# The scan's skip term, from two diagonal matmuls on TensorE to a row multiply and an addition on VectorE

## The chip, the cores and the metric

The kernel runs on one core of a Trainium2 chip. Its time is the device time of one execution in microseconds; lower is better. Three runs of the kernel before gave 847.05, 847.98 and 848.30 us.

## The reference, cut to what matters

The input has 8 sequences of 512 tokens with 128 channels. Each passes a normalization, then two branches: a Mamba-2 block with an MLP behind it (`s`), and an attention block with a mixture of four experts behind it (`g`); the output is `x + s * silu(g)`. The change touches the Mamba-2 part alone. It has 4 heads of 64 channels (256 in all) and a state of 64 per channel:

```python
xBC = silu(conv(xBC))                  # xs: 4 heads x 64, Bm: 64, Cm: 64
def step(h, inp):                      # over the 512 tokens
    dA = exp(dt_t * A)                 # one number per head
    h = h * dA + (dt_t * x_t) B_t^T
    y = h C_t
y = ys + xs * D[None, None, :, None]   # D: one number per head. The skip connection
y = y * silu(z)
y = y * rsqrt(mean(y**2) + EPS) * norm_w
return y @ out_proj_w.T
```

## The kernel before, in words

The kernel works on one sequence at a time, in rounds. A round has a stage B and a stage A. Stage B(r) carries the tail of sequence r (output projections, experts, MLP) and the head of sequence r+1 (projections, convolution, the attention's maxima). Stage A(r) then does the attention's exponentials and weighted values, the scan, and the normalization of the next input. One loop of 7 rounds runs on each engine's own instruction stream; a round -1 without a tail stands before it and a last stage B behind it. So stage A runs 8 times. The order of work on each engine is written out by hand; engines meet only through semaphores.

Stage A has 24 steps `e`, four groups `g` of six units `u`. Each step is one block of attention scores: TensorE makes the scores (`exp_scores`, L519, and `exp_scores_of_four`, L535, tile `S`), ScalarE exponentiates them into `sb_pr` (L1136), GpSimd masks them (L1784), TensorE weighs the values with them (`weigh_values`, L549, tile `R` from `sb_pr`, `sb_va`). In the first six steps TensorE also makes the scores of which VectorE takes the last maxima (`max_scores`, L487; `maxima`, L1236, record L1242).

Beside each group runs one chunk of 128 tokens of the scan, so there are four chunks, c = g = 0 to 3. All matrices are computed for a chunk at once:

- `scan_inputs` (L606): TensorE turns the chunk's `xact` to tokens by channels, into bank `R[2]` (256 columns of x, 128 of B and C), and the product of B and C into its last 128 columns.
- `scan_products` (L1518): VectorE makes `xdt` = turned x times dt (L1525), copies B (L1528) and masks the product (`gm`, L1529).
- `segments` (L590): TensorE makes the sums of decays in bank `R[1]`; ScalarE exponentiates them into `es` (L1181). The segments of chunk c wait for the state of chunk c-1 (`h_sb`), since they share the bank.
- `scan_weights` (L1531): VectorE multiplies `es` and `gm` to `wm` (L1535).
- GpSimd makes `xw` from `xdt` (L1791), for the new state.
- `scan_outputs` (L619): TensorE writes bank `R[3]`. Columns 256 to 511 get the share of the state (C times `hst`, chunks 1 to 3 alone); columns 0 to 255 get first the skip, `xact` times a diagonal matrix of D (`diag_d`, two products), and on it `wm` times `xdt` for each head.
- `scan_combine` (L1539): VectorE weighs the state's share by `dec` (L1548), adds the rest (L1553) and multiplies by silu(z) into `yz` (L1556). In chunk 0 there is only the last of the three.
- `scan_state` (L1558): VectorE moves the new state into `hst` (L1561 in chunk 0, L1563 and L1568 in the others).
- `turn_y` (L643): TensorE turns `yz` for the output projection (L647).

VectorE's order within stage A is in the function `stage_a` (L1570): a step has, in this order, the combine, the maximum, the attention's values, the scan's products, the scan's weights, the state, then the two early normalizations (`xn`, L1589), the statistics of the next input (L1266, step 9), the sigmoid and the joins of the output (L1499 to L1516) and the norms (L1279). GpSimd's order has besides the masks the norms' powers (L1680 at step 17).

A matmul of fp32 operands appears as two records in the trace, with two weight loads. All records of TensorE made by the helper `mm` have the line L455, so they are told apart by their tiles.

Of the kernel before, what the change touches and what calls it, by code (L numbers as in the profile page):

```python
# [32 lines left out]
ALU = mybir.AluOpType  # L33
# [3 lines left out]
P = 128  # L37
B, L, D = 8, 512, 128
T = L // P
NH, HP, NS = 4, 64, 64  # L40
DI = NH * HP
# [52 lines left out]
def build(nc, x, weights, vectors, rows, consts, out):  # L94
    with ExitStack() as ctx:
        def sb(name, shape, dt=F32):
            return ctx.enter_context(nc.sbuf_tensor("sb_" + name, shape, dt))
# [6 lines left out]
        def signal(name, per_round, ahead=0):  # L104

            sem = ctx.enter_context(nc.semaphore(name))
            per[sem.name], lead[sem.name] = per_round, ahead
            made.append(sem)
            return sem

        def at(sem, r, k):


            return (r + 2 + lead[sem.name]) * per[sem.name] + k
# [9 lines left out]
        ones = cst[:, 3 * P:4 * P]  # L124
# [6 lines left out]
        wqk = sb("wqk", [P, AH, HD])  # L131
        neg_a = sb("neg_a", [P, NH])
        diag_d = sb("diag_d", [P, 2, P])

        def w(name):
            a, b = W_COLS[name]
# [34 lines left out]
        xact = sb("xact", [P, 3, L])  # L171
# [6 lines left out]
        dec = sb("dec", [P, 3, T, NH])  # L178
# [11 lines left out]
        xdt = sb("xdt", [P, 2, DI])  # L190
# [4 lines left out]
        yc = sb("yc", [P, 2, DI])  # L195
# [34 lines left out]
        R = [ps(f"R{i}", [P, L]) for i in range(4)]  # L230
# [20 lines left out]

        pool_set = signal("pool_set", 0)
        dve_set = signal("dve_set", 0)
        act_set = signal("act_set", 0)


# [88 lines left out]
        h1_sb = signal("h1_sb", 2)  # L345
        sv_sb = signal("sv_sb", 1)
        cs_sb = signal("cs_sb", 2)
        moe_sb = signal("moe_sb", T * E)
        gr_sb = signal("gr_sb", 1 + T)
        og_sb = signal("og_sb", 3)  # L350
# [1 line left out]
        xdt_sb = signal("xdt_sb", T)  # L352
        gm_sb = signal("gm_sb", T)
        wm_sb = signal("wm_sb", T)
        yc_sb = signal("yc_sb", 2 * (T - 1))
        yz_sb = signal("yz_sb", T)
        h_sb = signal("h_sb", 1 + 2 * (T - 2))
        stat_sb = signal("stat_sb", 2, 1)
# [94 lines left out]
        def _(pe):  # L453
            def mm(o, lhsT, rhs, start=True, stop=True):
                return pe.matmul(o, lhsT, rhs, start=start, stop=stop, skip_group_check=True)  # L455
# [163 lines left out]
            def scan_outputs(r, c):  # L619

                s = slice(c * P, (c + 1) * P)
                pe.wait_ge(xdt_sb, at(xdt_sb, r, c + 1))
                if c == 0:
                    pe.wait_ge(moe_sb, at(moe_sb, r, 2 * E))
                else:
                    pe.wait_ge(h_sb, at(h_sb, r, 2 * c - 1))
                    pe.wait_ge(ao_sb, at(ao_sb, r, 2 * c))
                    mm(R[3][:, DI:2 * DI], cT[:, s], hst[:], True, False)
                for n in range(2):
                    mm(R[3][:, n * P:(n + 1) * P], xact[:, n, s], diag_d[:, n, :], c == 0 and n == 0, False)  # L630
                pe.wait_ge(wm_sb, at(wm_sb, r, c + 1))
                for h in range(NH):
                    i = mm(R[3][:, h * HP:(h + 1) * HP], wm[:, c % 2, h, :],
                           xdt[:, c % 2, h * HP:(h + 1) * HP], False, True)
                i.then_inc(y_ps, 1)

            def new_state(r, c):
# [297 lines left out]
            pe.wait_ge(xab_sb, at(xab_sb, -2, 1))  # L935
            transposes(R[1], lambda t: xa[:, t, :]).then_inc(xaT_ps, 1)
            pe.wait_ge(wh_loaded, 16)
            pe.wait_ge(xbT_sb, at(xbT_sb, -1, 0))
            project_qkv(-1, 0)
            stage_b(-1, False, True)  # L940
# [278 lines left out]
        def _(dve):  # L1219
# [311 lines left out]
            def scan_weights(r, c):  # L1531
                dve.wait_ge(seg_sb, at(seg_sb, r, c + 1))
                dve.wait_ge(gm_sb, at(gm_sb, r, c + 1))
                dve.wait_ge(y_ps, at(y_ps, r, c - 1))
                stt(out=wm[:, c % 2], in0=es[:, c % 2], scalar=1.0,  # L1535
                    in1=gm[:, c % 2, :].unsqueeze(1).broadcast_to([P, NH, P]),
                    op0=ALU.min, op1=ALU.mult).then_inc(wm_sb, 1)

            def scan_combine(r, c):  # L1539

                dve.wait_ge(y_ps, at(y_ps, r, c + 1))
                dve.wait_ge(zs_sb, at(zs_sb, r, 1))
                dve.wait_ge(yT_ps, at(yT_ps, r, c - 1))
                dve.wait_ge(yss_sb, at(yss_sb, r, c - 1))
                if c == 0:
                    y = R[3][:, 0:DI]
                else:
                    tt(yc[:, 0, :].rearrange("p (h d) -> p h d", h=NH),  # L1548
                       R[3][:, DI:2 * DI].rearrange("p (h d) -> p h d", h=NH),
                       dec[:, 0, c, :].unsqueeze(2).broadcast_to([P, NH, HP]), ALU.mult)\  # L1550
                        .then_inc(yc_sb, 1)
                    dve.wait_ge(yc_sb, at(yc_sb, r, 2 * c - 1))
                    tt(yc[:, 1, :], R[3][:, 0:DI], yc[:, 0, :], ALU.add).then_inc(yc_sb, 1)  # L1553
                    dve.wait_ge(yc_sb, at(yc_sb, r, 2 * c))
                    y = yc[:, 1, :]
                tt(yz[:, c % 2, :], y, zraw[:, c, 0:DI], ALU.mult).then_inc(yz_sb, 1)  # L1556

            def scan_state(r, c):  # L1558
# [70 lines left out]
            dve.wait_ge(act_set, 1)  # L1629
            ts(neg_a[:], neg_a[:], -1.0, None, ALU.mult).then_inc(dve_set, 1)  # L1630
            norms(-2)
            dve.wait_ge(dve_set, 13)
            stage_b(-1, False, True)
            dve.wait_ge(wt_loaded, 16)
# [255 lines left out]
```

## Time and profile before

| | |
|---|---|
| median of three runs | 847.98 us |
| the profiled execution's own time | 848.16 us |
| its span, first to last instruction | 846.4 us |
| TensorE busy | 777.2 us (92%) |
| VectorE busy | 613.7 us (73%) |
| ScalarE busy | 510.2 us (60%) |
| GpSimd busy | 293.8 us (35%) |
| mean granted TensorE clock | 0.990 |

Busy time is an average over stages with different limits. A share of 92% does not say that TensorE decides everywhere; that is read from the chain of waits and from the timeline. In a timeline row the first number is the start, the second the length in us from the first of the merged instructions to the end of the last, `xN` the number merged; a bracket says how long the engine had been idle and what released it.

### The profile page before, as it was taken

The page shows a single profiled execution, that of the slowest core. Times are in us where ns is not written, and L with a number is a line of the kernel's source. Part 1 is how long each engine was busy: PE and PEld are TensorE (multiplying, and loading weights), DVE is VectorE, ACT ScalarE, POOL GpSimd, SP SyncE. Part 2 cuts the span into 40 slices and gives each one's busy share as a digit, 9 for nine tenths or more (in the row PEclk, how much of TensorE's full clock was granted, in tenths as well). Part 3 has the DMA queues.
Part 4 walks back from the last instruction along what each step waited for, and adds up shares of the span by engine and source line. Part 5 has one row for each costly group of instructions (what it writes and reads, how often), then busy time and mean ns, then how long its engine had stood idle before and what let it go on. Part 6 is the DMA issues. An engine that isn't in the chain of part 4 may idle for free.

```text
span 846.4 us, 18186 instructions
## 1 busy us (share of the span) xinstructions
PE 777.2 (92%) x5482; PEld 486.3 (57%) x5482; DVE 613.7 (73%) x1491; ACT 510.2 (60%) x968; POOL 293.8 (35%) x577
## 2 busy tenths in 40 slices
PE   2779999999999999999899999999999999999997
PEld 1555564756547565665647565475556656475646
DVE  2685569785887868787697868878587877978624
ACT  2426784577753775467845677537754678456662
POOL 5413534143512616036240445216160262404400
PEclk9998999999999999999999999999999999999999
DMA  4000000000000000000000000000000000000000
GB/s 169 2 8 15 14 1 2 9 16 26 0 2 13 28 3 0 8 13 26 0 0 8 14 25 0 2 7 27 11 0 8 13 27 0 0 8 14 26 0 13
DMA packets 15145, 11.73 MB, mean 14 GB/s; under 512 B 1040, under 2 KB 13968, under 8 KB 14992
## 3 DMA queue, kind: packets, MB, share of 16 engines
q1 hardware_dynamic: 15120, 11.43, 4.5%
q8 instruction: 12, 0.20, 0.1%
q14 instruction: 13, 0.11, 0.0%
HBM read 7.76 MB, written 2.10 MB: 12 GB/s over the span
## 4 chain that ended last, share of the span: by engine, by line
PE 54%; DVE 18%; issue 12%; ACT 10%; POOL 4%; DVEq 1%; POOLq 0%; ACTq 0%
PE R L455 33%; PE S L455 13%; DVE sb_mx L1242 9%; ACT sb_pr L1136 3%; PE S L460 3%; DVE sb_cv L1260 2%; POOL sb_pr L1784 2%; PE R L573 2%; POOL sb_lnv L1680 2%; PE R L460 1%; DVE sb_x L1478 1%; ACT sb_junk L1053 1%; DVE sb_rqk L1387 1%; ACT sb_sq L1034 1%; PE R L616 1%
## 5 line engine op out<-in xcount | busy, mean ns | idle before, releaser
L1136 ACT ACTIVATE sb_pr<-S 128x768 f32<-128x768 f32 (+1 forms) x192 | 161.9, 886 | 111.8 <-PE S L455 111.8
L1242 DVE TENSOR_REDUCE sb_mx<-S 128x2 f32<-128x256 f32 (+3 forms) x256 | 198.0, 818 | 32.9 <-PE S L455 31.9
L1784 POOL TENSOR_SCALAR_AFFINE_SELECT sb_pr<-sb_pr 128x256 f32<-128x256 f32 (+1 forms) x192 | 98.7, 519 | 145.3 <-ACT sb_pr L1136 144.0
L455 PE MATMUL R<-sb_pr,sb_va 128*32 128x512 f32 (+3 forms) x1024 | 88.8, 441 | 3.4 <-POOL sb_pr L1784 1.2
L455 PE MATMUL R<-sb_W,sb_pr 128*128 128x96 f32 (+1 forms) x512 | 69.5, 276 | 0.0
L455 PE MATMUL R<-sb_xfT,sb_W 128*128 128x512 f32 x144 | 69.2, 602 | 0.0
L1771 POOL TENSOR_TENSOR sb_seg_r<-sb_seg_v,sb_seg_head 128x512 fp32r<-128x512 f32 x8 | 8.3, 1040 | 174.7 <-ACT sb_seg_v L1167 174.7
L455 PE MATMUL S<-sb_kT,sb_qT 32*128 32x256 f32 (+3 forms) x512 | 56.7, 385 | 13.0 <-DVE sb_mx L1242 10.2
L455 PEld LDWEIGHTS R<-sb_W,sb_pr 128*128 128x128 f32 x512 | 63.5, 192 | 3.8 <-issue 3.5
L455 PEld LDWEIGHTS S<-sb_kT,sb_qT 32*128 32x128 f32 x512 | 27.6, 183 | 65.5 <-DVE sb_mx L1242 58.2
L455 PE MATMUL S<-sb_qT,sb_kT 32*128 32x256 f32 (+3 forms) x512 | 56.5, 385 | 7.6 <-ACT sb_pr L1136 7.6
L1478 DVE SCALAR_TENSOR_TENSOR sb_x<-R,sb_wts,sb_x 128x96 f32<-128x96 f32 x128 | 40.7, 318 | 17.4 <-PE R L455 13.0
L455 PEld LDWEIGHTS S<-sb_qT,sb_kT 32*128 32x128 f32 x512 | 27.3, 183 | 42.6 <-ACT sb_pr L1136 22.3
L455 PE MATMUL S<-sb_maskb,sb_identb 128*128 128x128 bf16 (+1 forms) x384 | 49.4, 241 | 0.0
L1230 DVE RECIPROCAL sb_rden<-R 128x16 f32<-128x16 f32 x32 | 8.2, 257 | 49.0 <-PE R L573 38.2
L999 ACT ACTIVATE sb_pr<-R 128x512 f32<-128x512 f32 x32 | 19.1, 598 | 39.3 <-PE R L455 39.2
L455 PEld LDWEIGHTS R<-sb_pr,sb_va 128*32 128x32 f32 x1024 | 23.6, 108 | 27.8 <-POOL sb_pr L1784 9.4
L460 PE MATMUL S<-sb_cst,sb_tokqk 128*128 128x128 f32 x256 | 34.1, 294 | 4.2 <-DVE sb_tokqk L1428 2.2
L1694 POOL TENSOR_TENSOR sb_qk<-sb_qk,sb_wqk 128x512 f32<-128x512 f32 x8 | 10.2, 1270 | 75.6 <-ACT sb_sq L1034 75.6
L455 PEld LDWEIGHTS S<-sb_maskb,sb_identb 128*128 128x128 bf16 x384 | 23.8, 98 | 21.4 <-issue 17.7
L1260 DVE SCALAR_TENSOR_TENSOR sb_cv<-sb_xc,sb_vec,sb_cv 128x512 f32<-128x512 f32 x48 | 34.9, 728 | 0.0
L460 PEld LDWEIGHTS S<-sb_cst,sb_tokqk 128*128 128x128 f32 x256 | 31.0, 152 | 6.4 <-ACT sb_qT L1086 2.8
(230 smaller groups left out, 1726.1 us busy)
## 6 DMA issues: line engine op xcount, KB each, us to landing
sb_xin<-x SPq DMA_DIRECT2D x9, 256.0 KB, 2.8
sb_W<-weights SPq DMA_DIRECT2D x1, 2290.0 KB, 10.4
sb_qT<-sb_mT SPq DMA_DIRECT2D x128, 4.0 KB
sb_xres<-x SPq DMA_DIRECT2D x8, 256.0 KB, 2.8
out<-sb_xres SPq DMA_DIRECT2D x7, 256.0 KB, 2.3
sb_cT<-sb_xact SPq DMA_DIRECT2D x8, 128.0 KB, 2.3
sb_W<-weights SPq DMA_DIRECT2D x1, 514.0 KB, 4.6
sb_cst<-consts SPq DMA_DIRECT2D x1, 328.0 KB, 3.2
```

Source lines behind the costliest of these rows:

```text
L455: return pe.matmul(o, lhsT, rhs, start=start, stop=stop, skip_group_check=True)
L460: i = pe.transpose(o[:, t * P:(t + 1) * P], src(t), ident)
L573: i = pe.transpose(R[3][:, t * P:(t + 1) * P], oT[:, g % 2, t * P:(t + 1) * P], ident)
L616: pe.transpose(R[2][:, n * P:(n + 1) * P], xact[:, n, s], ident)
L999: act.activation(dst, R[k % 4][:, :], func, bias=bias).then_inc(act_up, 1)
L1136: act.activation(pr[:, e % 4, :, 0:n], S[pair_of_exp(e)][:, :, 0:n], ACT.Exp).then_inc(p_sb, 1)
L1242: o = dve.tensor_reduce(mx[:, n // P - 1, g, heads[0]:heads[1] + 1], found[:, :, at_col:at_col + n], AX.X, ALU.max, negate=True)
L1260: stt(out=cv[:, n], in0=xc[:, n, k:k + L], scalar=vcol(V_CONVW + TAPS * n + k), in1=cv[:, n], op0=ALU.mult, op1=ALU.add).then_inc(conv_dve, 1)
L1478: stt(out=x2[:, t, MASKED:D], in0=R[(22 + t) % 4][:, e * OC:(e + 1) * OC], scalar=wts[:, t, e:e + 1], in1=x2[:, t, MASKED:D], op0=ALU.mult ...
L1680: tt(lnv[:, 6:8, :].rearrange("p a t -> p (a t)"), lnv[:, 4:6, :].rearrange("p a t -> p (a t)"), minus_half[:], ALU.pow).then_inc(rn_sb, 1)
L1694: tt(qk[:, :, 0].rearrange("p t h d -> p t (h d)"), qk[:, :, 0].rearrange("p t h d -> p t (h d)"), wqk[:].rearrange("p h d -> p (h d)").un ...
L1784: pool.affine_select(out=keep, in_=keep, compare_op=ALU.is_ge, fill=0.0, base=0, pattern=pattern, channel_multiplier=-1)\
```

## The change

The skip is no longer part of the accumulation in `R[3]`. Before the loop, TensorE multiplies a matrix of ones by `diag_d`, which gives D as a row on all partitions; VectorE copies it to `drow`. In each chunk VectorE multiplies the turned x in `R[2]` by that row into `xd`, right behind `wm`. In chunk 0 the combine adds `xd` to the outputs; in the other chunks the product of the state's share with `dec` becomes four scalar_tensor_tensor, one for each head with 64 columns, that multiply by the head's decay and add `xd`. The first product of the heads starts the bank's accumulation in chunk 0.

```diff
         diag_d = sb("diag_d", [P, 2, P])
+        drow = sb("drow", [P, DI])
+        xd = sb("xd", [P, DI])
...
-                for n in range(2):
-                    mm(R[3][:, n * P:(n + 1) * P], xact[:, n, s], diag_d[:, n, :], c == 0 and n == 0, False)
                 pe.wait_ge(wm_sb, at(wm_sb, r, c + 1))
                 for h in range(NH):
                     i = mm(R[3][:, h * HP:(h + 1) * HP], wm[:, c % 2, h, :],
-                           xdt[:, c % 2, h * HP:(h + 1) * HP], False, True)
+                           xdt[:, c % 2, h * HP:(h + 1) * HP], c == 0 and h == 0, True)
...
             pe.wait_ge(wh_loaded, 16)
+            for n in range(2):
+                i = mm(R[0][:, n * P:(n + 1) * P], ones, diag_d[:, n, :])
+            i.then_inc(drow_ps, 1)
+            pe.wait_ge(drow_set, 1)
             pe.wait_ge(xbT_sb, at(xbT_sb, -1, 0))
             project_qkv(-1, 0)
...
                     in1=gm[:, c % 2, :].unsqueeze(1).broadcast_to([P, NH, P]),
                     op0=ALU.min, op1=ALU.mult).then_inc(wm_sb, 1)
+                tt(xd[:], R[2][:, 0:DI], drow[:], ALU.mult).then_inc(xd_sb, 1)
...
-                if c == 0:
-                    y = R[3][:, 0:DI]
-                else:
-                    tt(yc[:, 0, :].rearrange("p (h d) -> p h d", h=NH),
-                       R[3][:, DI:2 * DI].rearrange("p (h d) -> p h d", h=NH),
-                       dec[:, 0, c, :].unsqueeze(2).broadcast_to([P, NH, HP]), ALU.mult)\
-                        .then_inc(yc_sb, 1)
-                    dve.wait_ge(yc_sb, at(yc_sb, r, 2 * c - 1))
-                    tt(yc[:, 1, :], R[3][:, 0:DI], yc[:, 0, :], ALU.add).then_inc(yc_sb, 1)
+                skip = xd[:]
+                dve.wait_ge(xd_sb, at(xd_sb, r, c + 1))
+                if c > 0:
+                    for h in range(NH):
+                        hs = slice(h * HP, (h + 1) * HP)
+                        i = stt(out=yc[:, 0, hs], in0=R[3][:, DI + h * HP:DI + (h + 1) * HP],
+                                scalar=dec[:, 0, c, h:h + 1], in1=xd[:, hs], op0=ALU.mult, op1=ALU.add)
+                    i.then_inc(yc_sb, 1)
                     dve.wait_ge(yc_sb, at(yc_sb, r, 2 * c))
-                    y = yc[:, 1, :]
+                    skip = yc[:, 0, :]
+                tt(yc[:, 1, :], R[3][:, 0:DI], skip, ALU.add).then_inc(yc_sb, 1)
+                dve.wait_ge(yc_sb, at(yc_sb, r, 2 * c + 1))
+                y = yc[:, 1, :]
                 tt(yz[:, c % 2, :], y, zraw[:, c, 0:DI], ALU.mult).then_inc(yz_sb, 1)
...
             norms(-2)
+            dve.wait_ge(drow_ps, 1)
+            dve.tensor_copy(drow[:], R[0][:, 0:DI]).then_inc(drow_set, 1)
+            dve.wait_ge(drow_set, 1)
```

## Rows read from the trace of the kernel before

**Rows 1.** The page, busy time of each engine, share of the span, instructions.

```profile
PE 777.2 (92%) x5482; PEld 486.3 (57%) x5482; DVE 613.7 (73%) x1491; ACT 510.2 (60%) x968; POOL 293.8 (35%) x577
```

**Rows 2.** The page, the chain that ended last, by engine.

```profile
PE 54%; DVE 18%; issue 12%; ACT 10%; POOL 4%; DVEq 1%; POOLq 0%; ACTq 0%
```

**Rows 3.** Groups by line and form: count, busy us, mean ns, idle before.

```profile
L455 PE MATMUL R<-sb_diag_d,sb_xact 128*128 128x128 f32 x128 | 19.5, 275 | 0.0
...
L1548 DVE TENSOR_TENSOR sb_yc<-R,sb_dec 128x256 f32<-128x256 f32 x24 | 10.2, 425 | 20.8 <-PE R L455 19.8
...
L1373 DVE SCALAR_TENSOR_TENSOR sb_x<-R,sb_ry,sb_xn 128x128 f32<-128x128 f32 x32 | 9.0, 345 | 15.5 <-PE R L455 15.5
```

**Rows 4.** Timeline, VectorE instructions out of PSUM: start us, length us.

```profile
379.98 0.42 DVE L1525 TENSOR_TENSOR sb_xdt<-R,sb_dt 128x256 f32<-128x256 f32 x1
380.32 0.21 DVE L1528 COPY sb_btok<-R 128x64 f32<-128x64 f32 x1
...
406.74 1.13 DVE L1373 SCALAR_TENSOR_TENSOR sb_x<-R,sb_ry,sb_xn 128x128 f32<-128x128 f32 x4 [2.02 <-PE R L455]
```

**Rows 5.** Timeline, chunk 0 of one round.

```profile
369.54 0.95 DVE L1242 TENSOR_REDUCE sb_mx<-S 128x2 f32<-128x768 f32 x1
...
370.55 0.45 PE L455 MATMUL S<-sb_kT,sb_qT 32*128 32x256 f32 x4
...
371.15 0.61 PE L455 MATMUL R<-sb_diag_d,sb_xact 128*128 128x128 f32 x4
...
371.60 1.00 PE L455 MATMUL R<-sb_xdt,sb_wm 128*128 128x64 f32 x8
...
372.80 0.42 DVE L1556 TENSOR_TENSOR sb_yz<-R,sb_zraw 128x256 f32<-128x256 f32 x1
...
373.35 1.02 DVE L1242 TENSOR_REDUCE sb_mx<-S 128x2 f32<-128x512 f32 x2
...
374.60 0.51 PE L455 MATMUL S<-sb_qT,sb_kT 32*128 32x512 f32 x4
```

**Rows 6.** Timeline, chunk 1 of the same round.

```profile
380.83 0.82 DVE L1535 SCALAR_TENSOR_TENSOR sb_wm<-sb_es,sb_gm 128x512 f32<-128x512 f32 x1
...
381.62 0.61 PE L455 MATMUL R<-sb_diag_d,sb_xact 128*128 128x128 f32 x4
...
383.10 0.43 DVE L1548 TENSOR_TENSOR sb_yc<-R,sb_dec 128x256 f32<-128x256 f32 x1
...
384.81 0.42 DVE L1568 TENSOR_TENSOR sb_hst<-R,sb_hdec 64x256 f32<-64x256 f32 x1
...
385.28 0.50 PE L455 MATMUL R<-sb_seg_r,sb_seg_l 128*128 128x512 f32 x1
...
386.12 0.45 PE L455 MATMUL S<-sb_qT,sb_kT 32*128 32x384 f32 x4 [0.34 <-ACT sb_pr L1136]
...
386.70 1.06 PE L455 MATMUL R<-sb_pr,sb_va 128*32 128x512 f32 x8
```

**Rows 7.** Timeline, chunk 2 of the same round.

```profile
387.73 0.69 DVE L1512 TENSOR_TENSOR sb_gs<-sb_x,sb_gs 128x512 f32<-128x512 f32 x1
...
389.45 0.61 POOL L1791 TENSOR_TENSOR sb_xw<-sb_xdt,sb_dec 128x256 f32<-128x256 f32 x1 [0.25 <-DVE sb_xdt L1525]
...
390.32 1.83 POOL L1784 TENSOR_SCALAR_AFFINE_SELECT sb_pr<-sb_pr 128x512 f32<-128x512 f32 x2 [0.25 <-ACT sb_pr L1136]
...
392.12 1.64 POOL L1680 TENSOR_TENSOR sb_lnv<-sb_lnv,sb_minus_half 128x8 f32<-128x8 f32 x1
```

**Rows 8.** Timeline, the end of chunk 3 of the same round.

```profile
402.83 0.41 PE L647 MATMUL R<-sb_cst,sb_yz 128*128 128x128 f32 x2
```

**Rows 9.** Timeline, the first projection of the execution.

```profile
16.62 4.94 PE L455 MATMUL S<-sb_W,sb_xbT 128*128 128x384 f32 x8 [1.54 <-ACT sb_xbT L993]
```

**Rows 10.** Windows: us, busy of PE, PEld, DVE, ACT, POOL, granted clock, DMA share, GB/s.

```profile
312.00:316.00 4.00, 2.75 (x15) 1.76 (x14) 3.73 (x11) 3.15 (x15) 0.00 (x0) 1.00 0.00 0
316.00:320.00 4.00, 3.62 (x21) 3.19 (x20) 2.90 (x10) 4.00 (x8) 1.35 (x4) 0.73 0.00 0
```

More of the change, by code:

```diff
@@ L253, in build @@
         dve_set = signal("dve_set", 0)
+        drow_ps = signal("drow_ps", 0)
+        drow_set = signal("drow_set", 0)
         act_set = signal("act_set", 0)
@@ L347, in build @@
         cs_sb = signal("cs_sb", 2)
+        xd_sb = signal("xd_sb", T)
         moe_sb = signal("moe_sb", T * E)
@@ L354, in build @@
         wm_sb = signal("wm_sb", T)
-        yc_sb = signal("yc_sb", 2 * (T - 1))
+        yc_sb = signal("yc_sb", 1 + 2 * (T - 1))
         yz_sb = signal("yz_sb", T)
```

## The prediction

> **What bounds the kernel now.** I read the page's busy shares first. TensorE works 777.2 of 846.4 us and VectorE 613.7 [rows 1]; a change that takes work from the fuller engine and gives it to the emptier one looks good by that row alone. The chain of waits is the better guide: TensorE holds 54% of it, VectorE 18%, issue 12%, ScalarE 10% [rows 2]. So more than a third of the time is set by something other than TensorE. The question is whether the scan is in that part. For that I went through the timeline of one round's stage A, chunk by chunk, asking at each TensorE instruction what came last ahead of it. The round whose stage A lies at 363 to 403 us stands for all eight.
>
> **What is removed.** A 128x128 fp32 matmul is two records, so the skip is 4 records a chunk, 128 in all, 19.5 us busy by the records' own lengths [rows 3]. They overlap, however. In chunk 0 the four start at 371.15 and the next product starts at 371.60 [rows 5]: 0.45 us of TensorE's stream per chunk, 4 x 8 x 0.45 = 14.4 us in all. That is the most that can be gained.
>
> **What is added on VectorE.** Price by start-to-start distance, not by length. Each chunk gets `xd`, a 256-wide product out of PSUM. The 256-wide product of L1525 starts at 379.98 and the next independent instruction at 380.32 [rows 4]: 0.34 us. Chunk 0 gets one more 256-wide addition that the weighing waits for. I price it at its 0.425 us length [rows 3] plus some 0.035 us for the wait (chunk 0's L1556 is as long): 0.46 us. In chunks 1 to 3 one 256-wide product of 0.425 us becomes four 64-wide scalar_tensor_tensor. No row has that form at 64 columns. Four of them at 128 columns take 1.13 us [rows 4], one 0.345 us [rows 3], so the distance is (1.13 - 0.345) / 3 = 0.262 us; 64 columns fewer take 0.07 us off, an estimate from (0.425 - 0.21) us for 256 against 64 columns, a third of it (L1548 [rows 3], L1528 [rows 4]: 0.072). That gives a distance of 0.195 and a length of 0.275 us; four last 3 x 0.195 + 0.275 = 0.86 us, 0.44 more than now. Bounds: at a distance of 0.13 us (0.34 for 256 columns less 3 x 0.07) 0.67 us, and at 0.345 us (a full 128-wide length, nothing overlapped) 1.31 us. I take 0.86, from the nearest row in kind. Per round VectorE gets 4 x 0.34 + 0.46 + 3 x 0.44 = 3.1 us, 25 us in all: 1.7 times what TensorE loses.
>
> The rows show an independent VectorE instruction starting 0.08 us before the one in front has ended (0.42 long, 0.34 apart) [rows 4]. The Trainium skill, "VectorE: DVE Perf Modes", section "The DRAIN you can't avoid", says that the next instruction does not start until the pipe is empty, and its rules advise to lower the number of instructions. The trace disagrees with the first and agrees with the second; the four slices would by the first be 4 x 0.275 = 1.10 us, which is a rival below. In the same page, section "The TRN2 errata", a VectorE instruction out of PSUM is given 120 cycles plus its columns at 0.96 GHz; an estimate from that page makes four 64-wide ones 0.77 us against 0.39 for one of 256, +0.38 where I take +0.44.
>
> **Chunk 0.** After `wm`, VectorE starts the maximum of L1242 at 369.54 and it ends at 370.49; TensorE's next maximum scores, which wait for it, start at 370.55 [rows 5]. There is no slack, so `xd` (+0.34) moves both. TensorE then gets 0.45 us back by the missing skip and is on time again, but the next maximum on VectorE is +0.34, and it was followed by two `xn` instructions, the combine at 372.80 and the last maximum at 373.35 [rows 5]. VectorE could have started that one at 372.80 + 0.34 = 373.14, so 0.21 us of slack. With the extra addition: 0.34 + 0.46 - 0.21 = 0.59 late, end at 374.96 in place of 374.37. The exponent's scores at 374.60 [rows 5] wait for it; they had 374.60 - 374.37 - 0.06 (the wait's own time, as 370.49 to 370.55) = 0.17 us of slack. Chunk 0: +0.42 us.
>
> **Chunk 1.** TensorE gains 0.35 us (the outputs would start at 381.62, the skip's place, but `wm` ends at 380.83 + 0.82 = 381.65 and they wait 0.09 us for it [rows 6]). VectorE is solid from `xdt` to the new state: it inserts `xd` ahead of the statistics, +0.34, less 0.13 us that it idled before 383.10 [rows 6], and the slices +0.44. The state `hst`, 384.81 + 0.42 = 385.23 before, comes 0.65 us later, at 385.88. The segments (385.28 [rows 6]) wait for it, and behind them in TensorE's queue stand the scores at 386.12, held by ScalarE. They would follow the segments by about 0.5 us, at 386.42: +0.30. The values at 386.70 [rows 6] were held by GpSimd, 386.70 - (386.12 + 0.45) = 0.13 us later than the scores alone would have it: +0.15 us. So what TensorE gained is not only lost, the sign turns.
>
> **Chunk 2.** VectorE enters it with its two joins; L1512 starts at 387.73 and has no gap ahead of or behind it [rows 7], so the 0.65 us stay. `xdt` comes at about 389.6, and GpSimd's `xw`, which waits for it (389.45 to 390.06 before), ends at 390.7, after the affine select that starts at 390.32 should have begun [rows 7]. Behind it in GpSimd's queue are a second select and the power at 392.12, which lies on the chain of waits. The two selects take 1.83 us beside VectorE's L1516; in part they will now lie elsewhere. Between 0 and +0.45 us beyond chunk 1; I take +0.15. The 0.45 us of TensorE buy nothing here, since GpSimd sets the end.
>
> **Chunk 3.** The outputs are done 0.44 us earlier, the slices take 0.44 more, and `yz`, which the turning of y at 402.83 waits for, ends where it did [rows 8]. 0 us.
>
> **Start.** Two small matmuls, a copy and a wait come before the first projection at 16.62, which waits 1.5 us for ScalarE's `xbT` [rows 9]; the new work lies beside that. 0 to 0.2 us. If that cover were gone it would cost about 1.3 us, once.
>
> **Sum.** 0.42 + 0.15 + 0.15 = 0.72 us a round, 8 rounds: 5.8 us. The profiled execution took 848.16 us (span 846.4 and 1.76 around it), 0.18 above the median: 848.16 + 5.8 = 854.0 us.
>
> **The clock.** In one round of the profile TensorE is granted 0.73 of its full clock over 316 to 320 us, so half of that stretch was at 1.2 GHz; in the 4 us before it worked 2.75 us of 4 [rows 10]. Were TensorE the bound there, it would cost 4 x 0.27 = 1.1 us. The change shifts stage B against such stretches, so one or two may come fewer or more: -2.2 to +2.2 us, no part of the sum.
>
> **Rivals.**
> A. *TensorE decides, VectorE's additions are covered.* For it: the busy shares [rows 1]. Against it: in chunks 0 and 1 the waits above have slack under 0.2 us. It would give -0.1 (the maximum's 370.55 still holds), -0.35, 0 (GpSimd) and -0.4 us in the four chunks, -0.85 x 8 = -6.8: 841.4 us. It holds from the point where `xd` starts behind the maximum and not ahead of it, or VectorE's idle time before 383.10 exceeds 0.8 us. Chance 0.08.
> B. *The ties are looser than I read.* The 0.1 to 0.2 us slacks are each 0.1 larger and chunk 2's shift is absorbed: +0.2 in chunk 0, 0 after: 1.6 us, 849.8 us; with one low-clock stretch fewer, 848.7. Chance 0.17.
> C. *Slices end to end.* Each slice starts only when the one in front has ended, 0.275 us apart: +0.24 in each of chunks 1 to 3, all on the path: 8 x 0.72 = 5.8 more, 860 us. At 0.345 us it would be 8 x 3 x 0.45 = 10.8 more, 865 us. Against it, the distances in rows 4. Chance 0.12. This is what the Trainium skill's section on the DRAIN, named above, would have.
> D. *GpSimd pays fully in chunk 2*, +0.45 and not +0.15: 2.4 us more, 856.4. I count it within the forecast.
> That the change does not do what it says, I exclude: the skip's matmuls are gone from the code.
>
> **How the numbers follow.** Forecast (with D) 0.63, C 0.12, B 0.17, A 0.08. About 0.2%, 1.7 us, is what a measurement can tell from no change. Slower: all of the forecast and C, and half of B: 0.82. Same: the other half of B: 0.10. Faster: A: 0.08. The range reaches from B's middle, 849, to C's, 860.
>
> **What would show it.** Right: TensorE's idle before the maximum scores of chunk 0 grows by 0.3 us; the segments of chunk 1 wait for `hst`; `xw` starts late in chunk 2; a round 0.7 us longer; VectorE busy near 639 us. Wrong: `xd` under 0.3 us apart from its follower, the slices under 0.15 or over 0.25 us apart, or a stage A of unchanged length.

## The result and the profile after

The kernel after takes 851.72 us in the median of 8 runs (849.91 to 854.22), the kernel before beside it 847.93 (8 runs, 847.05 to 850.01). The ratio is 1.0049, 95% interval 1.0035 to 1.0063: slower by half a per cent. The profiled execution of after took 853.07 us (span 851.3, mean granted clock 0.990). That is 4.9 us above the profiled execution of before, where the medians are 3.8 apart. One program's single runs spread by some 4 us with the granted clock (0.986 in the run of 854.22, 0.995 in that of 849.91), so below I go by rounds in which the clock did not fall.

The page of after, busy time by engine, which answers to [rows 1]:

```profile
PE 772.5 (91%) x5358; PEld 471.3 (55%) x5358; DVE 634.2 (75%) x1604; ACT 511.5 (60%) x968; POOL 298.2 (35%) x577
```

TensorE lost 4.7 us and VectorE gained 20.5. The prediction had 25 us for VectorE (busy near 639 us, 634.2 measured); 2.3 of the missing us are the third join of the output, which got shorter in seven rounds (below). GpSimd, whose instructions are the same 577, gained 4.4 us: some of them take longer now.

The groups by line and form of after, where the new instructions and GpSimd's narrow mask stand (count, busy us, mean ns, idle before):

```profile
L1558 DVE SCALAR_TENSOR_TENSOR sb_yc<-R,sb_dec,sb_xd 128x64 f32<-128x64 f32 x96 | 20.7, 278 | 11.1 <-PE R L460 11.1
...
L1545 DVE TENSOR_TENSOR sb_xd<-R,sb_drow 128x256 f32<-128x256 f32 x32 | 13.3, 415 | 0.0
...
L1797 POOL TENSOR_SCALAR_AFFINE_SELECT sb_pr<-sb_pr 128x256 f32<-128x256 f32 x128 | 58.8, 461 | 102.9 <-ACT sb_pr L1143 102.8
```

A slice takes 278 ns (275 predicted), `xd` 415 (by its distance 340). The same narrow select took 415 ns in the kernel before: no line of it was changed, it only lies beside other work, mostly the first two joins. (A join is one of three 512-wide VectorE instructions with both inputs in SBUF that put the output together; steps 13 and 15.)

**By rounds.** I measure a round from one turning of the attention's values at the start of stage B to the next. An undisturbed round is 98.54 us before (four of the seven lie at 98.41 to 98.56, one at 98.83) and 99.16 after (six of the seven lie at 99.02 to 99.25): +0.62. The profiled difference of 4.91 splits into +0.62 up to the first mark, +2.57 over the seven rounds and +1.71 behind the last mark. Seven times 0.62 is 4.3; to it comes 1.1 of a round of after with a fallen clock, and 2.7 goes off since before had two such rounds; that leaves 2.7, and the small differences between rounds of before make it 2.57. The tail has a fallen clock in after alone.

The +0.62 up to the first mark is another thing than a round's. The first projection starts at 16.62 us in both kernels, but the first stage A starts at 66.43 before and at 66.76 after, +0.33, and is itself only 0.29 us longer. That stage A has no tail and so no joins, and its chunk 2 got shorter: 8.92 us before, 8.70 after.

**By chunk.** The timeline of after in the round shown before. Its stage A starts 1.25 us later (`scan_inputs` of chunk 0 at 366.45 for 365.20), so take 1.25 off to set a start beside [rows 5 to 8]. Chunk 0:

```profile
370.80 0.42 DVE L1545 TENSOR_TENSOR sb_xd<-R,sb_drow 128x256 f32<-128x256 f32 x1
371.13 0.95 DVE L1249 TENSOR_REDUCE sb_mx<-S 128x2 f32<-128x768 f32 x1
...
372.14 0.45 PE L460 MATMUL S<-sb_kT,sb_qT 32*128 32x256 f32 x4 [0.23 <-DVE sb_mx L1249]
...
374.39 0.42 DVE L1563 TENSOR_TENSOR sb_yc<-R,sb_xd 128x256 f32<-128x256 f32 x1
374.85 0.42 DVE L1566 TENSOR_TENSOR sb_yz<-sb_yc,sb_zraw 128x256 f32<-128x256 f32 x1
375.19 1.01 DVE L1249 TENSOR_REDUCE sb_mx<-S 128x2 f32<-128x512 f32 x2
376.26 0.51 PE L460 MATMUL S<-sb_qT,sb_kT 32*128 32x512 f32 x4
```

The maximum scores at 370.89 (372.14 less 1.25) were at 370.55 [rows 5]: +0.34, and TensorE now idles 0.23 us for the maximum. The exponent's scores at 375.01 were at 374.60: +0.41. Chunk 1:

```profile
382.48 0.82 DVE L1542 SCALAR_TENSOR_TENSOR sb_wm<-sb_es,sb_gm 128x512 f32<-128x512 f32 x1
...
383.36 1.10 PE L460 MATMUL R<-sb_xdt,sb_wm 128*128 128x64 f32 x8
...
384.89 0.86 DVE L1558 SCALAR_TENSOR_TENSOR sb_yc<-R,sb_dec,sb_xd 128x64 f32<-128x64 f32 x4
...
387.03 0.42 DVE L1578 TENSOR_TENSOR sb_hst<-R,sb_hdec 64x256 f32<-64x256 f32 x1
387.50 0.49 PE L460 MATMUL R<-sb_seg_r,sb_seg_l 128*128 128x512 f32 x1 [0.34 <-DVE sb_hst L1578]
...
387.93 0.44 PE L460 MATMUL S<-sb_qT,sb_kT 32*128 32x384 f32 x4
388.30 1.07 PE L460 MATMUL R<-sb_pr,sb_va 128*32 128x512 f32 x8
```

The four slices take 0.86 us, 0.19 apart. The segments wait 0.34 us for the state. But the scores follow the segments by 0.43 and the values follow the scores by 0.37, where they had stood 0.84 and 0.58 apart: the slack swallows nearly all. Chunk 2, VectorE's joins, GpSimd's queue and the three places where TensorE waits:

```profile
389.95 0.71 DVE L1519 TENSOR_TENSOR sb_gs<-sb_x,sb_gs 128x512 f32<-128x512 f32 x1
...
391.57 0.61 POOL L1804 TENSOR_TENSOR sb_xw<-sb_xdt,sb_dec 128x256 f32<-128x256 f32 x1 [0.65 <-DVE sb_xdt L1532]
...
391.92 0.82 DVE L1542 SCALAR_TENSOR_TENSOR sb_wm<-sb_es,sb_gm 128x512 f32<-128x512 f32 x1
392.14 2.13 POOL L1797 TENSOR_SCALAR_AFFINE_SELECT sb_pr<-sb_pr 128x512 f32<-128x512 f32 x2
392.79 1.10 PE L460 MATMUL R<-sb_xdt,sb_wm 128*128 128x64 f32 x8 [0.33 <-DVE sb_wm L1542]
392.99 0.78 DVE L1523 TENSOR_TENSOR sb_xres<-sb_gs,sb_xres 128x512 f32<-128x512 f32 x1
...
394.24 1.64 POOL L1693 TENSOR_TENSOR sb_lnv<-sb_lnv,sb_minus_half 128x8 f32<-128x8 f32 x1
...
396.63 0.47 PE L460 MATMUL R<-sb_seg_r,sb_seg_l 128*128 128x512 f32 x1 [0.43 <-DVE sb_hst L1578]
397.68 1.06 PE L460 MATMUL R<-sb_pr,sb_va 128*32 128x512 f32 x8 [0.20 <-POOL sb_pr L1797]
```

The same places in the kernel before (its weights `wm`, the outputs, the segments and the values; rows that stood in no group):

```profile
389.79 0.82 DVE L1535 SCALAR_TENSOR_TENSOR sb_wm<-sb_es,sb_gm 128x512 f32<-128x512 f32 x1
...
391.01 1.00 PE L455 MATMUL R<-sb_xdt,sb_wm 128*128 128x64 f32 x8
...
394.32 0.47 PE L455 MATMUL R<-sb_seg_r,sb_seg_l 128*128 128x512 f32 x1
...
395.69 1.06 PE L455 MATMUL R<-sb_pr,sb_va 128*32 128x512 f32 x8 [0.18 <-POOL sb_pr L1784]
```

GpSimd is late: its selects begin 0.57 us later (392.14 less 1.25 against 390.32 [rows 7]) and take 2.13 us instead of 1.83. But TensorE's outputs wait for VectorE, 0.33 us for `wm`, and its segments 0.43 us for the state (0.14 before, too short for a bracket); only the last values wait for GpSimd, 0.20 us against 0.18 before. The round shown and one other have a chunk 2 of 9.38 us; in the other five rounds of the loop and behind it, where that last wait is 0.10 us, it is 9.25 to 9.27. Chunk 3, its last answer to [rows 8]:

```profile
404.78 0.44 PE L650 MATMUL R<-sb_cst,sb_yz 128*128 128x128 f32 x2 [0.24 <-DVE sb_yz L1566]
```

All kernels in one table. "Round" is an undisturbed one; c0 to c3 are the four parts of stage A in the round shown (cut where chunk 0's scan inputs start and then at each turning of the attention's values, which stands right ahead of the next chunk's inputs; for e4 in the round behind it, since in the one shown its clock had fallen). Chunk 2 of after and of e3 is 9.25 to 9.28 in most rounds. Medians in us with the number of runs; ratios to the kernel before on the same chip, whose medians there were 848.33 (e1 to e4), 848.1 (e5 to e8) and 848.46 (e9 to e12).

| kernel | round | c0 | c1 | c2 | c3 | median (runs) | ratio [95%] |
|---|---|---|---|---|---|---|---|
| before | 98.54 | 13.53 | 8.97 | 8.99 | 6.69 | 847.93 (8) | |
| after | 99.16 | 13.93 | 8.92 | 9.38 | 6.68 | 851.72 (8) | 1.0049 [1.0035, 1.0063] |
| e1 no skip at all | 97.49 | 13.42 | 8.71 | 8.75 | 6.25 | 845.01 (7) | 0.9939 [0.9914, 0.9965] |
| e2 before, unused xd | 98.92 | 13.87 | 8.97 | 9.03 | 6.68 | 848.66 (10) | 1.0004 [0.9991, 1.0017] |
| e3 after, xd later | 98.80 | 13.61 | 8.90 | 9.38 | 6.68 | 848.62 (10) | 1.0001 [0.9990, 1.0012] |
| e4 after, one product | 98.41 | 13.93 | 8.71 | 9.18 | 6.24 | 848.34 (10) | 0.9989 [0.9974, 1.0003] |
| e5 e3, statistics and joins moved | 98.79 | 13.60 | 8.71 | 8.70 | 7.41 | 847.92 (10) | 0.9998 [0.9987, 1.0009] |
| e6 before, both moved | 99.01 | 13.54 | 8.96 | 9.47 | 6.69 | 850.75 (10) | 1.0025 [1.0013, 1.0037] |
| e7 after, joins moved | 99.32 | 13.93 | 8.92 | 8.74 | 7.40 | 852.91 (3) | 1.0047 [1.0027, 1.0066] |
| e8 e3, statistics moved | 98.54 | 13.60 | 8.71 | 9.22 | 6.68 | 848.64 (8) | 0.9994 [0.9981, 1.0008] |
| e9 e8, one join moved, filler | 98.52 | 13.59 | 8.70 | 9.22 | 6.68 | 849.17 (10) | 1.0000 [0.9991, 1.0010] |
| e10 before, filler | 98.55 | | | | | 848.49 (10) | 0.9998 [0.9987, 1.0010] |
| e11 after, filler | 99.13 | | | | | 851.51 (10) | 1.0043 [1.0028, 1.0058] |
| e12 before, e9's moves, filler | 99.06 | 13.55 | 8.97 | 9.50 | 6.69 | 850.97 (10) | 1.0025 [1.0011, 1.0039] |

### The profile page after: what moved, and what is told of

Read it like the earlier page. It is cut to its first block and busy times, and to the rows that moved or that the text cites. A ratio compares the mean times of both kernels' runs of the same rounds, so it can differ in the third digit from the quotient of the medians.

```text
span 851.3 us, 18101 instructions
## 1 busy us (share of the span) xinstructions
PE 772.5 (91%) x5358; PEld 471.3 (55%) x5358; DVE 634.2 (75%) x1604; ACT 511.5 (60%) x968; POOL 298.2 (35%) x577
## 5 line engine op out<-in xcount | busy, mean ns | idle before, releaser
L1797 POOL TENSOR_SCALAR_AFFINE_SELECT sb_pr<-sb_pr 128x256 f32<-128x256 f32 (+1 forms) x192 | 106.8, 561 | 142.3 <-ACT sb_pr L1143 142.0
L460 PEld LDWEIGHTS R<-sb_xdt,sb_wm 128*128 128x128 f32 x256 | 31.7, 191 | 8.5 <-DVE sb_wm L1542 8.0
L460 PE MATMUL R<-sb_xdt,sb_wm 128*128 128x64 f32 x256 | 33.7, 275 | 2.3 <-DVE sb_wm L1542 2.3
L465 PE MATMUL S<-sb_cst,sb_tokqk 128*128 128x128 f32 x256 | 31.2, 276 | 4.8 <-ACT sb_qT L1093 2.3
```

The costliest lines, as they stand in the source:

```text
L465: i = pe.transpose(o[:, t * P:(t + 1) * P], src(t), ident)
L1797: pool.affine_select(out=keep, in_=keep, compare_op=ALU.is_ge, fill=0.0, base=0, pattern=pattern, channel_multiplier=-1)\
```

## The experiments

**e1: what is the matmuls' going worth by itself?** The skip is left out of the kernel before.

```diff
-                for n in range(2):
-                    mm(R[3][:, n * P:(n + 1) * P], xact[:, n, s], diag_d[:, n, :], c == 0 and n == 0, False)
```

> The kernel before with the skip's two matmuls left out and nothing put in their place (the skip term is missing from the result). It prices what TensorE's relief is worth by itself. Theory (short slacks on VectorE and GpSimd decide): the undisturbed round, 98.54 us before, falls by 0.8 to 0.9 us, to 97.7: 0.1 in chunk 0, 0.35 in chunk 1, nothing in chunk 2 where GpSimd's power sets the end, 0.4 in chunk 3; about 841 us. Rival A (TensorE decides everywhere): it falls by the whole 4 x 0.45 = 1.8 us, to 96.8, 834 us. Rival V (VectorE decides everywhere): no change, 848 us.

A round is 1.05 us shorter, each chunk 0.11 to 0.44: a little more than expected, and the 0.24 of chunk 2 was not expected at all, there where I had held GpSimd to set the end. The median is 845.01 and not 841; the clock of the single runs is told at the end. Nothing new lies on VectorE, and this is what rival A would have kept of the 1.8 us of TensorE's stream. In chunk 3 `yz` now comes early enough, and the values are turned 0.44 us sooner.

From before to e1 it is -1.05, from e1 to after +1.67: VectorE's additions cost 1.67 us of the 3.1 they occupy.

**e2: what does `xd` cost where it stands?** The kernel before with its matmuls, and an `xd` that nobody reads.

```diff
                     op0=ALU.min, op1=ALU.mult).then_inc(wm_sb, 1)
+                tt(xd[:], R[2][:, 0:DI], cst[:, P:P + DI], ALU.mult).then_inc(xd_sb, 1)
```

> The kernel before with the skip still on TensorE; VectorE makes in each chunk, at the place of xd, a 256-wide product of the turned x that nobody reads. It adds 4 x 0.34 us a round to VectorE and takes nothing from TensorE. Theory: chunk 0 +0.34 us (the maximum behind it has no slack), chunk 1 close to 0, chunk 2 between 0 and +0.4 by GpSimd's xw, chunk 3 nothing: the undisturbed round +0.35 to +0.7, about 851 to 853 us. Rival A (TensorE decides): no change, 848 us.

+0.38 a round, 0.34 of it in chunk 0. The timeline of e2 (its stage A starts 0.48 us after that of before):

```profile
370.04 0.42 DVE L1540 TENSOR_TENSOR sb_xd<-R,sb_cst 128x256 f32<-128x256 f32 x1
370.37 0.95 DVE L1244 TENSOR_REDUCE sb_mx<-S 128x2 f32<-128x768 f32 x1
371.37 0.44 PE L457 MATMUL S<-sb_kT,sb_qT 32*128 32x256 f32 x4 [0.34 <-DVE sb_mx L1244]
```

`xd` puts the maximum off by 0.33 us (370.37 less 0.48 against 369.54 [rows 5]) and TensorE waits for it: the tie of chunk 0 is as tight as read. In chunks 1 to 3 an `xd` by itself is nearly free (0, +0.04, -0.01). The round is as expected, the median is not: 0.33 us above before, where 8 x 0.38 would give 3.0. The granted clock was 0.988 to 0.994 here and 0.984 to 0.991 in before's runs beside it.

**e3: is its place the cause?** After, with chunk 0's `xd` behind the maximum and two of the `xn`, where VectorE had slack.

```diff
+                if c:
+                    skip_term()
+
+            def skip_term():
                 tt(xd[:], R[2][:, 0:DI], drow[:], ALU.mult).then_inc(xd_sb, 1)
...
+                    if e == 3:
+                        skip_term()
```

> The changed kernel, only chunk 0's xd moved behind the maximum and the two xn of step 3, where VectorE idled 0.35 us. Theory: chunk 0's +0.41 us falls to about +0.1, the undisturbed round from 99.16 to 98.85, 849.5 us at the same clock. Rival (chunk 0's loss comes from the extra addition and not from where xd stands): no change, 99.16.

Chunk 0 falls from 13.93 to 13.61, the round by 0.36. The timeline of e3:

```profile
371.21 0.95 DVE L1249 TENSOR_REDUCE sb_mx<-S 128x2 f32<-128x768 f32 x1
...
372.22 0.45 PE L460 MATMUL S<-sb_kT,sb_qT 32*128 32x256 f32 x4
372.59 0.42 DVE L1549 TENSOR_TENSOR sb_xd<-R,sb_drow 128x256 f32<-128x256 f32 x1
373.03 1.02 DVE L1249 TENSOR_REDUCE sb_mx<-S 128x2 f32<-128x512 f32 x2
```

TensorE's scores no longer wait in this row. With one instruction elsewhere more than half of the loss is gone, 0.36 of 0.62, and the median is level with before.

**e4: what do the four slices cost?** After, with the single product of before in chunks 1 to 3.

```diff
                 if c > 0:
-                    for h in range(NH):
-                        hs = slice(h * HP, (h + 1) * HP)
-                        i = stt(out=yc[:, 0, hs], in0=R[3][:, DI + h * HP:DI + (h + 1) * HP],
-                                scalar=dec[:, 0, c, h:h + 1], in1=xd[:, hs], op0=ALU.mult, op1=ALU.add)
-                    i.then_inc(yc_sb, 1)
+                    tt(yc[:, 0, :].rearrange("p (h d) -> p h d", h=NH),
+                       R[3][:, DI:2 * DI].rearrange("p (h d) -> p h d", h=NH),
+                       dec[:, 0, c, :].unsqueeze(2).broadcast_to([P, NH, HP]), ALU.mult)\
+                        .then_inc(yc_sb, 1)
```

> The changed kernel with the four 64-wide slices of chunks 1 to 3 replaced by the one 256-wide product of before, so the skip term is missing there; xd is still made. It prices the slices: VectorE 0.43 us less in each of three chunks. Theory: chunk 1 gains 0.2 to 0.3 (the segments' wait for the state goes), chunk 2 0.2 to 0.4 (VectorE and xw earlier), chunk 3 0.4 (yz earlier): the undisturbed round from 99.16 to 98.2, about 844 us. Rival G (only GpSimd's late xw counts, chunk 3 is covered): to 98.8. Rival C0 (the loss is all chunk 0): no change.

-0.75 a round, a little less than the 0.96 expected: 0.21, 0.20 and 0.44 in the three chunks by the table, 0.09 in chunk 2 in most rounds. So chunk 1 does pay for its slices, and the 0 of chunk 3 is made of +0.44 for them and -0.44 for the matmuls. The median shows less than 8 times 0.75, since in the profiled execution every second round had a fallen clock and was 1.1 us longer. GpSimd's selects in chunk 2 of another round of e4:

```profile
490.90 2.13 POOL L1796 TENSOR_SCALAR_AFFINE_SELECT sb_pr<-sb_pr 128x512 f32<-128x512 f32 x2
```

The selects stay at 2.13 us without the slices, so another thing stretches them.

**e5 to e8: what stretches chunk 2, and can it be avoided?** The suspects are VectorE's three joins. The first two stand ahead of chunk 2's `xdt` in VectorE's order, the third lies beside the selects. e7 moves them behind the last chunk's combine, in after; e5 does that with e3's place of `xd` and with the statistics of the next input at step 7; e8 is e5 without the joins' move; e6 gives both moves to the kernel before.

```diff
-JOIN_AT = {13: (0, 1), 15: (2,)}
+JOIN_AT = {19: (0, 1, 2)}
-STATS_AT = 9
+STATS_AT = 7
```

> The changed kernel with three moves on VectorE alone: chunk 0's xd behind the maximum (as in the run before), the statistics from step 9 to step 7 (VectorE idled 2 us there) and the three joins from steps 13 and 15 to step 19 (it idled 2 us there too). No instruction more or fewer. Theory: chunk 0 about +0.1 against before, chunk 1 -0.35 (the state is no longer late), chunk 2 -0.3 to -0.5 (xw on time, the selects alone), chunk 3 0: the undisturbed round 97.7 to 98.0, so 842 to 844 us at an undisturbed clock. Rival (the moved work makes VectorE late elsewhere, above all in chunk 3): 98.8 or more.

> The kernel before, skip on TensorE, with the same two moves of the statistics and the joins. Theory: TensorE and ScalarE set the end where VectorE now has room, so next to nothing: undisturbed round 98.3 to 98.6. Then the skip's move is worth about -0.6 us a round in this order of work, where it costs +0.6 in the given one. Rival (the gain of the run above is all the moves' own): 97.8 as well.

> The changed kernel with the three joins alone moved to step 19. Theory: VectorE enters chunk 2 0.6 us earlier, xw is on time and the two selects take about 1.4 and not 2.1 us, so chunk 2's +0.4 us goes: undisturbed round 98.5 to 98.75. Rival (chunk 2's loss is the clock's or TensorE's, not GpSimd's): 99.16 unchanged.

> The changed kernel with chunk 0's xd behind the maximum and the statistics at step 7, joins where they were. Theory: chunk 1's state comes about 0.7 us earlier and VectorE enters the joins earlier, so chunk 2's shift shrinks too: undisturbed round from 98.80 to 98.2 to 98.5. Rival (only the joins count): 98.80 unchanged.

e7 against after: chunk 2 -0.64 (-0.54 in most rounds), chunk 3 +0.72. The joins' place was the cause, as the first stage A had hinted, and moving them only moves the loss: e7's round is 0.16 us longer, where a gain of about 0.5 was expected, and e5 came out at its rival's 98.79. The timeline of e7 in chunks 2 and 3:

```profile
391.79 0.82 DVE L1542 SCALAR_TENSOR_TENSOR sb_wm<-sb_es,sb_gm 128x512 f32<-128x512 f32 x1
...
392.66 1.10 PE L460 MATMUL R<-sb_xdt,sb_wm 128*128 128x64 f32 x8
...
402.28 1.10 PE L460 MATMUL R<-sb_xdt,sb_wm 128*128 128x64 f32 x8 [0.46 <-DVE sb_wm L1542]
```

The scan's inputs of chunk 2 start at 390.19 in e7 and at 389.79 in after. The outputs start 2.48 us behind them in e7 and wait for nothing; in after it is 3.00, with the wait for `wm`. These 0.52 us are the gain. In chunk 3 it is the other way round: there the joins now stand ahead of `xdt`, and TensorE waits 0.46 us for `wm`, where after has no wait. So the joins cost by making VectorE late.

**What stretches the selects** is a second thing. The pair in e5, with the joins gone:

```profile
390.19 1.38 POOL L1803 TENSOR_SCALAR_AFFINE_SELECT sb_pr<-sb_pr 128x512 f32<-128x512 f32 x2 [0.25 <-ACT sb_pr L1143]
```

It takes 1.38 us there, 1.83 in before and 2.13 in after. e9, below, has the first two joins in place and only the third one gone:

```profile
388.31 0.82 DVE L1544 SCALAR_TENSOR_TENSOR sb_wm<-sb_es,sb_gm 128x512 f32<-128x512 f32 x1
388.53 1.68 POOL L1805 TENSOR_SCALAR_AFFINE_SELECT sb_pr<-sb_pr 128x512 f32<-128x512 f32 x2
...
389.18 1.10 PE L460 MATMUL R<-sb_xdt,sb_wm 128*128 128x64 f32 x8 [0.33 <-DVE sb_wm L1544]
...
390.18 1.64 POOL L1701 TENSOR_TENSOR sb_lnv<-sb_lnv,sb_minus_half 128x8 f32<-128x8 f32 x1
```

So the third join is worth 2.13 - 1.68 = 0.45 us of the pair, and the same in before (1.83 - 1.38). The 0.30 us that after adds is `wm`, also a VectorE product of two SBUF inputs: the pair lies beside it for 0.60 us in after and e9 and for 0.29 or 0.30 in before and e5 (389.79 + 0.82 less 390.32), since `wm` came 0.53 us later in the chunk than in before and the selects only 0.23. The third join takes 0.68 us alone, 0.78 in after and 1.12 in before, where it starts inside a select:

```profile
390.54 1.12 DVE L1516 TENSOR_TENSOR sb_xres<-sb_gs,sb_xres 128x512 f32<-128x512 f32 x1
```

And the pair's length is worth next to nothing here: e9 differs from e8 by the third join (and a filler that changes no round, below), its power comes 0.44 us earlier in the chunk, and chunk 2 is 9.19 to 9.23 in both.

e8's earlier statistics gain 0.19 in chunk 1 and 0.05 in chunk 2 (0.16 in the round shown) against e3, since the state comes sooner: 98.54 a round, before's own and just short of what was expected. e6 was a miss. I had expected next to nothing, and the moves cost the kernel before 0.47 a round, all of it in chunk 2: a select beside the first join, for which TensorE waits (as in e12 below):

```profile
395.57 1.06 PE L455 MATMUL R<-sb_pr,sb_va 128*32 128x512 f32 x8 [0.69 <-POOL sb_pr L1784]
```

In the moved order the skip on VectorE (with chunk 0's `xd` behind the maximum) is the faster one, 98.79 against 99.01; in the given order it is slower, 98.80 against 98.54 with `xd` there and 99.16 where the change had put it.

**e9 to e12: one join later, and the clock.** In before the fallen clock lies mostly in stage B, where TensorE idles 0.93 us for the second normalization. The filler gives it two matmuls that nobody reads.

```diff
                 if tail:
+                    if head:
+                        dense(R[0][:, 0:256], 2)
                     pe.wait_ge(x1n_sb, at(x1n_sb, r, 1))
```

e9 has it with e8's order and the third join alone at step 19, e10 with before, e11 with after, e12 with before and e9's two moved constants:

```diff
-JOIN_AT = {13: (0, 1), 15: (2,)}
+JOIN_AT = {13: (0, 1), 19: (2,)}
-STATS_AT = 9
+STATS_AT = 7
```

> The changed kernel with chunk 0's xd behind the maximum, the statistics at step 7, the first two joins where they were and only the third at step 19, behind the norms and outside chunk 2; and two idle 256-wide matmuls of constants into a free bank ahead of TensorE's wait for x1n in stage B, 0.75 us in a gap of 0.93 us, so that they delay nothing. Theory: the third join no longer lies beside GpSimd's two selects of chunk 2 (1.4 us, not 1.8 to 2.1), so the undisturbed round is 98.1 to 98.4, where 98.54 stood without these two edits; and the stretches of low clock in stage B go or get rare, so all runs lie near 843 to 845 us. Rival (the clock falls for another reason than that gap): single runs still 1.3 us apart in steps, clock 0.988 to 0.992, median over 847.

> The kernel before with only the two idle matmuls ahead of the wait for x1n. Theory: undisturbed round 98.54 as before, but the one or two low-clock rounds go: 846 us and less spread. Rival (gap is not the cause): 848, unchanged.

> The changed kernel with only the two idle matmuls. Theory: undisturbed round 99.16; without low-clock rounds the run takes 8 x 0.61 = 4.9 us more than the kernel before with the same two matmuls, some 851 us. Rival: the change costs the measured 3.8 us whatever the clock does.

> The kernel before (skip on TensorE) with the same moves of the statistics and the third join and the same two idle matmuls. Theory: it has no late state in chunk 1, so the statistics bring nothing or cost up to 0.2 us; the third join gives back up to 0.3 us in chunk 2: undisturbed round 98.3 to 98.6, at or above that of the changed kernel with the same moves by 0 to 0.4 us. Rival (the moves alone make the gain, the skip's place none): lower than that of the changed kernel.

The filler changes nothing: e10 and e11 repeat before and after, round and median, and the fallen stretches stay. So the gap it fills is not their cause. The third join gains nothing beyond e8 either, so e9 (98.52 a round, 849.17 us) missed both its round and its time; what is late in its chunk 2 is `wm` (above) and the state once more:

```profile
393.02 0.47 PE L460 MATMUL R<-sb_seg_r,sb_seg_l 128*128 128x512 f32 x1 [0.43 <-DVE sb_hst L1584]
```

e12, too, missed what was expected (99.06 for 98.3 to 98.6), and shows why: one narrow select and one join beside it, and TensorE waiting:

```profile
400.61 0.97 POOL L1786 TENSOR_SCALAR_AFFINE_SELECT sb_pr<-sb_pr 128x256 f32<-128x256 f32 x1 [0.49 <-ACT sb_pr L1138]
400.63 0.68 DVE L1518 TENSOR_TENSOR sb_xres<-sb_gs,sb_xres 128x512 f32<-128x512 f32 x1
...
401.63 1.07 PE L455 MATMUL R<-sb_pr,sb_va 128*32 128x512 f32 x8 [0.68 <-POOL sb_pr L1786]
...
402.07 0.41 POOL L1786 TENSOR_SCALAR_AFFINE_SELECT sb_pr<-sb_pr 128x256 f32<-128x256 f32 x1 [0.50 <-ACT sb_pr L1138]
```

The select takes 0.97 us instead of 0.41, and TensorE waits 0.68 us for it. e9 and e12 have one order and differ in the skip and in `xd`'s place: 98.52 against 99.06.

No version that computes the whole is faster than before: the lowest ratio, e8's 0.9994, has an interval that holds 1.

## Why the prediction was right, and which term was not

| step | predicted, us a round | measured |
|---|---|---|
| `xd` to its follower | 0.34 | 0.33 |
| four slices | 0.86, 0.195 apart | 0.86, 0.19 apart |
| chunk 0 | +0.42 | +0.40 |
| chunk 1 | +0.15 | -0.05 |
| chunk 2 | +0.15, bounds 0 and 0.45 beyond chunk 1 | +0.39 in the round shown, +0.28 in most |
| chunk 3 | 0 | -0.01 |
| start | 0 to 0.2, once | +0.33 at the first stage A |
| sum | 0.72 | 0.73 in the round shown, 0.62 over the rounds |
| whole | +5.8 (854.0) | +4.9 profiled, +3.8 in the medians |

**The direction and its ground held; that the sums agree is luck.** Chunk 1 came 0.20 us lower than its term and chunk 2 0.13 to 0.24 higher, and chunk 2 for another reason than the one given. Nor does the round shown stand for all eight: the first has no joins. VectorE, at 73% the emptier engine, set the times in stage A. e1 shows that the full engine's relief is worth 1.05 us a round when nothing is added, and e2 that one 0.42 us instruction on the emptier one takes 0.38 back. Rival A failed at the condition that it was given: `xd` starts ahead of the maximum. e3 puts it behind, and the loss falls to 0.26, though it does not turn into the 6.8 us gain of A, since the slices are still there.

**Chunk 0** was right in every link: 0.34 to the scores, the addition 0.46 long with its wait, 0.41 at the exponent's scores.

**Chunk 1's term was too high.** The chain I followed is there (the segments wait 0.34 us for `hst`), but its three distances were each a little long. Beside chunk 0's shift of 0.40, the state is 0.57 us late where I had 0.65. The scores follow the segments by 0.43, not 0.5, and the values the scores by 0.37, not 0.43. Together 0.2 us. e4 (0.21 less without the slices) shows that the slices reach the end of this chunk; the missing matmuls pay for them.

**Chunk 2's term was inside its bounds, but its path was the wrong one.** The step that failed is "The 0.45 us of TensorE buy nothing here, since GpSimd sets the end". Without the skip's matmuls chunk 2 is 0.24 us shorter (e1), and in the first stage A, which has no joins, it is 0.22 us shorter in after itself. What sets it in after is VectorE: it comes out of the joins late, the outputs wait 0.33 us for `wm`, which the prediction did not look at in this chunk, and behind the slices the segments wait 0.43 us for the state. `xw` was late and the selects behind it, as predicted; that the joins "in part will now lie elsewhere" was wrong, for the pair got 0.30 us longer. (The trace has 0.10 us of idle ahead of L1512 where the prediction read none; nothing hangs on it.) But the selects are GpSimd's side, and e9 against e8 shows that 0.44 us less of it changes the chunk by some 0.02. So rival D, "GpSimd pays fully", is near in size (0.28 to 0.39 for 0.45) and wrong in its mechanism.

**Chunk 3** was right, and e4 shows both halves of its zero. **The start** was not 0 in effect. The first projection stands at 16.62 in both kernels; in after it waits 0.69 us for ScalarE in place of 1.54 [rows 9], so the cover held there. Yet the first stage A starts 0.33 us later. The traces of e6 and e10, which start as before does, have it at 66.20 and 66.23, and those of e5, e7, e8 and e9, which start as after does, at 66.61 to 66.75; the six others have it at 67.58 or later, in either form. Where the third of a microsecond arises is open.

**Rival C** is refuted by the slices' distance: 0.19 us, not 0.278. The Trainium skill, "VectorE: DVE Perf Modes", has in its section "Two Vector instructions with no wait between them" what decides it: an instruction is held until those in front have finished if one of its tensors starts in another group of 32 partitions than the last one did in that memory. All tensors here start at partition 0, so by that section nothing is held, and the trace agrees (0.42 us long, 0.33 apart). I had weighed only the sentence on the DRAIN, which that section qualifies. **Rival B** was right for chunk 1 and wrong for chunk 0 and 2. By the time alone, 851.72 lies between its 849.8 and the forecast's 854.0, 1.9 us above the one and 2.3 below the other. By the chunks, and by the profiled execution on which the sum was built (853.07), the forecast is the nearer.

**What the total does not explain.** The undisturbed rounds and the start give 7 x 0.62 + 0.33 + 0.29 = 5.0 us, the medians 3.8. Before's own runs differ by 2 us and after's by 4 with their clock, and a round with a fallen stretch was 1.1 to 1.4 us longer. That after had on average one stretch fewer fits, but I did not show it. I had kept the clock out of the sum at -2.2 to +2.2.

## What to carry to other kernels

Busy shares say which engine could decide, not which one does: at each instruction of the fuller engine ask what it last waited for, and count work moved to the emptier one in full wherever that wait has no slack. Where a new instruction stands costs as much as what it is: `xd` ahead of a maximum cost 0.36 us a round more than three instructions later. With it there the same change is 0.26 us a round slower in the given order and 0.54 faster in that of e9 and e12; but that order serves the kernel before badly, and the best round of either form is the same 98.5. When a change shifts a queue, instructions that nobody touched can get longer, as GpSimd's did beside VectorE's products. Before calling that the cause, look at what the fuller engine waits for: here it was mostly VectorE itself, late behind work that stood ahead in its queue.

## What was not expected of the hardware

**A join beside a select.** GpSimd's 256-wide select took 0.41 us alone and 0.97 beside a 0.68 us VectorE product of two SBUF inputs (e12); a 512-wide one takes 0.63 alone and 1.08 beside the third join, in before and in after. The lengths follow a pattern: in before and after, a 512-wide select that starts beside such a product ends 0.49 to 0.50 us behind the product's end (62 cases), in after a 256-wide one 0.26 to 0.27 us behind it (14 cases), and a 0.68 us product that starts inside a select ends 0.54 to 0.55 us behind the select's end (21 cases). Whichever comes second keeps all but some 0.14 us of its own length for the time behind the other. The Trainium skill, "SBUF — State Buffer", sections "SBUF: two separate sides" and "Who interferes with whom", says that a VectorE instruction with two SBUF inputs and a GpSimd one that reads SBUF meet on a shared port pair, that the one which starts first has it for its whole length, and that the other is fully blocked. The trace agrees but for those 0.14 us: in e12 the select gained 0.56 of the product's 0.68 us and ends 0.27 us after it, where full blocking would leave about 0.39; there the two start 0.02 us apart, so which was first can't be told. No run here shows by itself that the port is the reason.

**The clock of one program differs from run to run.** Single runs of e1, one program, took 837.66 and 839.03 us at a mean granted clock of 0.992, 843.30 at 0.986 and four 845.01 to 845.64 at 0.982: 8 us apart. Over 85 runs of the kernel before, 53 at a clock of 0.990 average 847.95 us, 20 at 0.988 849.80 and 6 at 0.984 850.91. The fallen stretches lie in stage B or at its edges in before (316 to 324 and 612 to 620) and in stage A and the tail in after. Windows of after (us, busy of PE, PEld, DVE, ACT, POOL, granted clock, DMA share, GB/s):

```profile
172.00:176.00 4.00, 3.78 (x34) 2.57 (x30) 3.62 (x10) 1.62 (x2) 0.94 (x3) 0.94 0.00 0
176.00:180.00 4.00, 4.00 (x34) 1.53 (x34) 3.58 (x8) 1.49 (x2) 0.68 (x2) 0.63 0.22 66
...
812.00:816.00 4.00, 3.66 (x13) 2.20 (x13) 1.96 (x12) 2.25 (x4) 0.00 (x0) 0.73 0.02 4
816.00:820.00 4.00, 4.00 (x9) 1.68 (x8) 1.42 (x8) 2.96 (x6) 0.00 (x0) 0.85 0.00 0
```

At 176 to 180 us most of the stretch was at 1.2 GHz, although TensorE had worked 3.78 of the 4 us in front, in which the granted clock was already 0.94. What makes it fall there stays open; that the 0.93 us gap in stage B is the cause is ruled out by e10 and e11. For a reader it means that e1's true worth shows in its rounds (8 x 1.05 = 8.4 us, and its two best runs are 9 to 11 us under before), while its median shows 3.3.
